# State-space block with a quantized feed-forward on one core: drives as float32 products with diagonals of B, and operands turned by transposing DMAs

## What is computed

```
# state-space part, per batch b, channel e (256), state n (16), time l (256)
xin = in_proj_w @ ctx.T ; u = silu(causal_conv4(xin) + conv_b)
dt_lo, B, C = x_proj_w @ u                       # 8, 16 and 16 rows
delta = softplus(dt_proj_w @ dt_lo + dt_proj_b)
state[e,n] = state[e,n] * exp(delta*A[e,n]) + (delta*u)[e] * B[n]   # over l
y[e] = sum_n state[e,n]*C[n] + D[e]*u[e]
x = x + tanh(g_xattn) * (y * silu(layernorm(x)))
# feed-forward part
t = layernorm(x); q = quantize per token (8 bits)
gate, up = q @ ternary(w_gate).T, q @ ternary(w_up).T
h = hadamard(silu(gate)*up)  (1024 wide);  q2 = quantize per token
x = x + tanh(g_ffn) * (q2 @ ternary(w_down).T)
```

## Time and profile before

| what | us |
|---|---|
| median of 3 runs (lowest, highest) | 222.16 (221.88, 225.17) |
| the profiled execution, its own time | 223.4 |
| its span, from first to last instruction | 221.6 |
| busy PE / PEld | 167.9 / 136.7 |
| busy DVE | 188.3 |
| busy ACT | 172.8 |
| busy POOL | 148.5 |

### The profile page before, as it was taken

One profiled execution on the slowest core, in us unless ns is written; L12 is line 12 of the kernel. 1 busy time (PEld: TensorE's weight loads), 2 busy tenths in 40 slices (PEclk: granted clock), 3 DMA queues, 4 the chain that ended last, 5 costly groups with the idle time before them and its releaser, 6 DMA issues.

```text
span 221.6 us, 3745 instructions
## 1 busy us (share of the span) xinstructions
PE 167.9 (76%) x1216; PEld 136.7 (62%) x1216; DVE 188.3 (85%) x292; ACT 172.8 (78%) x302; POOL 148.5 (67%) x247
## 2 busy tenths in 40 slices
PE   2757475997897994979867968988587598677873
PEld 1535354796695984748757864877484487544751
DVE  3462889597999999999999899999979996889983
ACT  0699997799899989799879895999497630985373
POOL 1103039969787989999999999999995299510000
PEclk9965587579999999999999999999999999999999
DMA  4994000000000000000000000000000000000001
GB/s 77 315 355 165 1 0 1 0 4 0 0 3 0 0 3 0 0 4 0 1 0 4 0 0 27 0 3 23 0 1 4 24 0 27 0 0 0 24 27 47
DMA packets 8148, 6.33 MB, mean 29 GB/s; under 512 B 2202, under 2 KB 7874, under 8 KB 8130
## 3 DMA queue, kind: packets, MB, share of 16 engines
q1 hardware_dynamic: 7154, 6.02, 8.6%
q10 hardware_dynamic: 976, 0.09, 0.3%
HBM read 5.05 MB, written 1.05 MB: 28 GB/s over the span
## 4 chain that ended last, share of the span: by engine, by line
POOL 25%; DVE 11%; PE 11%; ACT 8%; issue 4%; POOLq 0%; DVEq 0%; ACTq 0%
POOL driveT L1413 7%; POOL wnat L1479 7%; POOL wnat L1478 7%; PE GP L601 2%; DVE wnat L1789 2%; ACT L1242 2%; PE PY L483 2%; PE BC L422 1%; DVE wnat L1792 1%; DVE wnat L1730 1%; DVE prod L1686 1%; DVE state L1609 1%; PE UP L422 1%; ACT xn L1163 1%; DVE wnat L1778 1%
## 5 line engine op out<-in xcount | busy, mean ns | idle before, releaser
L1413 POOL TENSOR_SCALAR driveT<-duT,BT 128x256 f32<-128x256 f32 x120 | 58.4, 506 | 14.6 <-ACT duT L1071 11.9
L1054 ACT ACTIVATE decay<-delta,zero_c,aneg 128x255 f32<-128x255 f32 x128 | 65.0, 588 | 0.1
L1686 DVE TENSOR_TENSOR prod<-state,BC 128x1024 f32<-128x1024 f32 x32 | 38.5, 1202 | 3.2 <-PE BC L467 2.7
L1609 DVE TENSOR_TENSOR_SCAN state<-decay,BC 128x512 f32<-128x512 f32 x30 | 36.4, 1212 | 2.0 <-ACT decay L1054 1.2
L1609 DVE TENSOR_TENSOR_SCAN state<-decay,UP 128x512 f32<-128x512 f32 x30 | 35.9, 1198 | 0.0
L483 PE MATMUL PY<-id,prod 128*128 128x128 f32 x256 | 33.0, 273 | 0.8 <-DVE prod L1686 0.5
L483 PEld LDWEIGHTS PY<-id,prod 128*128 128x128 f32 x256 | 28.7, 140 | 1.8 <-issue 0.8
L1478 POOL TENSOR_TENSOR wnat<-wnat 128x512 f32<-128x512 f32 x18 | 22.9, 1271 | 8.0 <-DVE wnat L1730 7.2
L422 PE MATMUL BC<-id,driveT 128*128 128x128 f32 x120 | 19.4, 286 | 8.2 <-POOL driveT L1413 4.4
L1479 POOL TENSOR_TENSOR wnat<-wnat 128x512 f32<-128x512 f32 x18 | 22.9, 1272 | 0.0
L422 PEld LDWEIGHTS BC<-id,driveT 128*128 128x128 f32 x120 | 14.4, 148 | 11.9 <-issue 5.5
(11 more groups left out here) (254 smaller groups left out, 392.0 us busy)
## 6 DMA issues: line engine op xcount, KB each, us to landing
wnat<-in_L_ffn_w_gate_dram SPq DMA_DIRECT2D x1, 1024.0 KB, 6.4
xs<-in_x_dram SPq DMA_DIRECT2D x1, 1024.0 KB, 8.8
wnat<-in_L_ffn_w_up_dram SPq DMA_DIRECT2D x1, 1024.0 KB, 11.2
wnat<-in_L_ffn_w_down_dram SPq DMA_DIRECT2D x1, 1024.0 KB, 11.2
out_dram<-ot SPq DMA_DIRECT2D x8, 128.0 KB, 1.7
ctxs<-in_ctx_dram SPq DMA_DIRECT2D x1, 384.0 KB, 3.8
ctxs<-in_ctx_dram SPq DMA_DIRECT2D x1, 128.0 KB, 2.8
inw<-n_L_xattn_in_proj_w_dram SPq DMA_DIRECT2D x1, 128.0 KB, 2.6
```

The lines of the kernel that those rows point to most:

```text
L1054: last = nc.scalar.activation(decay[:, m % RING, h, n, 1:L], delta[:, b % 2, h, 1:L], ACT.Exp, bias=zero_c[:], scale=aneg[:, h, NB * j + n ...
L1413: last = nc.gpsimd.tensor_scalar(driveT[:, m % RING, c, n], duT[:, b % 2, c], BT[:, b % 2, c, NB * j + n:NB * j + n + 1], 1.0, ALU.mult, A ...
L1609: nc.vector.tensor_tensor_scan(state[:, g % STATES, h].rearrange("p n l -> p (n l)"), decay[:, g % RING, h].rearrange("p n l -> p (n l)"), ...
L1686: nc.vector.tensor_tensor(prod[:, g % RING].rearrange("p h n l -> p h (n l)"), state[:, g % STATES].rearrange("p h n l -> p h (n l)"), PC. ...
```

## The change

1. *Drives.* For every quarter of a batch (four states) POOL builds with one `affine_select` diagonal matrices of B: 128 x 1024 floats, 16 such instructions in all (`diagonals`). `drive_rows` is now a float32 product of `duT` (stationary) with two diagonals at a time (moving, 256 columns), two such products per half and step. The 120 POOL multiplications and the 240 transposes go, and so does the separate way of steps 0 and 1 (`B_rows`, `copy_B`, `first_drive`).
2. *Turning.* The weights are clipped from below in SBUF (`weight_floor`, DVE, 128 x 2048 16-bit) and turned by SP's transposing DMAs from SBUF to SBUF (`turn_weights`), 512 KB each. The tokens (`turn_tokens`, 128 KB) and the rounded operand of the down product (`turn_down`, 256 KB) of batches 0, 1, 2 (down: 0, 1) go the same way. `weight_T`, `weight_out`, `tokens_T`, `tokens_out_early` and four of six `q2_T` with their copies go. Batch 3's tokens and the down operands of batches 2 and 3 are still turned by PE.
3. *Front.* Small loads move from SP to ACT's queue; x is loaded ahead of the gate weight; a table load moves under the first loads; the first tap is a Copy without the bias, which goes into the Silu; two Relu move to DVE; the sum of the weights' absolute values comes after softplus(0).
4. *Order.* `decays` counts per half, and the lists of all engines are new.

The core of the diff (setups, semaphore names and most of the new lists left out):

```diff
@@ SP
+            def turn_weights(m):
+                sp.wait_ge(dve_wq, m + 1)
+                sp.dma_start(wT[:, m].rearrange("p (k c) -> p k c", c=P), wq[:, m], transpose=True).then_inc(turned_w, 16)
+            def turn_tokens(f):
+                sp.wait_ge(dve_q, f + 1)
+                if f >= 1:
+                    sp.wait_ge(pe_up, LC * f)
+                sp.dma_start(qT[:].rearrange("p t h c -> p (t h) c"), q[:].rearrange("p t e -> p (t e)"), transpose=True
+                             ).then_inc(turned_q, 16)
+            def turn_down(f, t):
+                sp.wait_ge(dve_q2, LC * f + t + 1)
...
+                sp.dma_start(q2T[:, t], q2[:, t], transpose=True).then_inc(turned_d[t], 16)
+            turn_tokens(0)
+            turn_weights(0)
+            turn_weights(1)
+            turn_weights(2)
+            turn_down(0, 0)
+            turn_tokens(1)
+            store(0, 0)
+            turn_down(0, 1)
+            turn_down(1, 0)
+            store(0, 1)
+            turn_tokens(2)
+            turn_down(1, 1)
...
@@ PE
+            def drive_rows(m, h):
...
+                pe.wait_ge(act_duT, b + 1)
+                pe.wait_ge(pool_diagB, m * NB // PER + 1)
...
+                for c in range(LC):
+                    last = nc.tensor.matmul(drive_bank(h).rearrange("p (n c l) -> p n c l", n=NB, c=LC)[:, :, c, :],
+                                            duT[:, b % 2, c, P * h:P * (h + 1)], diagB[:, q, c, at:at + NB, :],
                                             start=True, stop=True)
...
             def gate(f, t):
-                pe.wait_ge(act_qT, f + 1)
+                pe.wait_ge(turned_q, 16 * (f + 1))
                 if f == 0 and t == 0:
-                    pe.wait_ge(dve_wT, 6)
+                    pe.wait_ge(turned_w, 16 * 3)
+                    pe.wait_ge(act_spread, 2)
                     pe.wait_ge(act_duT, 2)
...
+            drive_rows(12, 0)
+            drive_rows(12, 1)
+            accumulate(10)
+            gate(0, 0)
             C_rows(11)
             drive_rows(13, 0)
...
@@ POOL
+            def diagonals(n, i):
+                pool.wait_ge(act_BT, n + 1)
+                if n >= 1:
+                    pool.wait_ge(pe_drive, HALF * (STEPS * (n - 1) + (i + 1) * PER // NB))
+                nc.gpsimd.affine_select(diagB[:, i].rearrange("p c n l -> p (c n) l"),
+                                        BT[:, n % 2, i].rearrange("p c n -> p (c n)").unsqueeze(2).to_broadcast([P, LC * PER, P]),
+                                        [[0, LC * PER], [1, P]], ALU.is_equal, no_part, base=0,
+                                        channel_multiplier=-1).then_inc(pool_diagB, 1)
@@ DVE
+            def weight_floor(m):
+                dve.wait_ge(dve_wr, m + 1)
+                nc.vector.tensor_scalar(wq[:, m], wq[:, m], -1.0, None, ALU.max).then_inc(dve_wq, 1)
...
             times_C(10)
-            token_scale(0, dve_ln_link)
-            weight_out(4)
-            weight_out(5)
+            weight_floor(2)
             round_tokens(0)
             scan(12, 0)
             scan(12, 1)
             times_C(11)
```

More of the change, by code:

```diff
@@ L764, in _ @@
             in_proj(1, 1)
+            drive_rows(0, 0)
+            drive_rows(0, 1)
+            x_dbl(1)
+            drive_rows(1, 0)
+            drive_rows(1, 1)
+            dt_proj(1)
             drive_rows(2, 0)
             drive_rows(2, 1)
-            x_dbl(1)
             drive_rows(3, 0)
@@ L770, in _ @@
             drive_rows(3, 1)
-            dt_proj(1)
+            gate_T(0)
+            in_proj(2, 0)
             C_rows(2)
@@ L830, in _ @@
             du_T(2)
-            C_rows(12)
-            gate(0, 1)
-            x_dbl(3)
-            drive_rows(14, 0)
             drive_rows(14, 1)
+            up(0, 1)
             C_rows(13)
-            up(0, 0)
+            accumulate(11)
             drive_rows(15, 0)
-            up(0, 1)
             drive_rows(15, 1)
             C_rows(14)
-            accumulate(10)
+            accumulate(12)
             drive_rows(16, 0)
+            accumulate(13)
+            x_dbl(3)
             drive_rows(16, 1)
-            accumulate(11)
+            accumulate(14)
@@ L846, in _ @@
             C_rows(15)
-            accumulate(12)
             drive_rows(17, 0)
-            accumulate(13)
             drive_rows(17, 1)
-            accumulate(14)
-            dt_proj(3)
+            inter_T(0, 0)
             C_rows(16)
-            accumulate(15)
-            C_rows(17)
             drive_rows(18, 0)
             drive_rows(18, 1)
+            accumulate(15)
+            dt_proj(3)
+            C_rows(17)
+            hadamard_mm(0, 0)
             drive_rows(19, 0)
-            inter_T(0, 0)
+            accumulate(16)
@@ L860, in _ @@
+            C_rows(18)
             drive_rows(19, 1)
-            C_rows(18)
-            hadamard_mm(0, 0)
+            inter_T(0, 1)
+            gate_T(2)
             drive_rows(20, 0)
-            accumulate(16)
-            gate_T(2)
+            C_rows(19)
             drive_rows(20, 1)
-            C_rows(19)
+            down(0, 0)
+            drive_rows(21, 0)
             accumulate(17)
-            accumulate(18)
-            inter_T(0, 1)
-            drive_rows(21, 0)
-            C_rows(20)
@@ L889, in _ @@
             drive_rows(24, 0)
+            C_rows(22)
             accumulate(20)
             drive_rows(24, 1)
+            down(0, 1)
             accumulate(21)
-            q2_T(0, 1)
             C_rows(23)
+            drive_rows(25, 0)
+            up(1, 1)
             accumulate(22)
-            up(1, 1)
-            drive_rows(25, 0)
             drive_rows(25, 1)
-            down(0, 1)
             accumulate(23)
@@ L1083, in silu_u @@
                     act.wait_ge(dve_conv, 2 * (DC - 1))
-                    nc.scalar.activation(u[:, 0], conv[:], ACT.Silu, bias=zero_c[:]).then_inc(act_u, 1)
+                    act.wait_ge(ld_cb, 16)
+                    for h in range(HALF):
+                        last = nc.scalar.activation(u[:, 0, h], conv[:, h], ACT.Silu, bias=cb[:, h:h + 1])
+                    last.then_inc(act_u, 1)
                 elif n == 1:
@@ new lines, in _ @@
+            inter_out(0, 0)
+            decays(21, 1)
+            spread(3)
+            decays(22, 0)
+            softplus(3)
+            quant_down(0, 0)
+            rstd2(1)
+            decays(22, 1)
+            inter_out(0, 1)
+            decays(23, 0)
+            second_norm(1)
+            scale_tokens(1)
+            decays(23, 1)
+            gate_out(2)
+            decays(24, 0)
+            quant_down(0, 1)
+            for_silu()
+            silu_gate(1, 0)
+            silu_z(3)
@@ L1364, in _ @@
+            decays(30, 0)
+            scale_tokens(2)
+            decays(30, 1)
+            quant_down(1, 1)
+            for_silu()
             silu_gate(2, 0)
@@ L1906, in _ @@
             weight_round(0)
-            weight_round(1)
-            weight_out(0)
             scan(7, 1)
             times_C(6)
-            weight_out(1)
+            weight_floor(0)
+            weight_round(1)
             scan(8, 0)
@@ L1915, in _ @@
             scan(9, 0)
-            weight_round(2)
             scan(9, 1)
-            weight_out(2)
+            weight_floor(1)
+            residual(0)
             times_C(8)
-            residual(0)
-            weight_out(3)
             scan(10, 0)
```

640 lines of the change are left out of this document (280 added, 360 removed).

## The result

| kernel | median us (lowest, highest) | ratio, 95% interval | profiled span |
|---|---|---|---|
| before, beside the changed one | 223.66 (221.88, 225.86) | | 221.6 |
| changed | 241.25 (241.15, 242.23) | 1.0808 [1.075, 1.0866] | 239.5 |

The change makes the kernel 8% slower, where the forecast had 4%. Between the profiles lie 17.9 us. The profiles of the eighth and the ninth experiment were taken in executions over 1.5% above the fastest of their kernel, so their later milestones aren't set beside others.

A forecast was written before the change was run, and what follows sets the result against it. DVE was taken as the bound, with PE 94% full after the change. Terms -6.8 + 2.5 + 8.5 + 1.5 + 1.7 + 3 - 1 = +9.4 us gave 231.5 us against 222.16; range 219 to 245.

The forecast's parts named there:

- the tail: End of the kernel: the same but for the order of a few PE calls, 0 us (-1 to +1).
- the gap: Sign: a DVE gap of 5 us or more ahead of times_C(11), at step 12.
- the dip of the clock: After PE's idle time at gate(0, 0): lower granted clock makes two steps' drives twice as long, +1.5 us (0 to 4).
- the pace of the drives: Sign: drives show as 8 PE instructions a step, 0.215 us apart.
- Part 1: Drives: PE pays 1.73 us a step against 0.88, 94% full from gate(0, 0) on; +3 us (0 to 6) there.
- My upper end: Four turns ahead of gate(0, 0), in 256-byte rows: 6656 packets at 43 ns, 19.4 us with the landing.
- -6.8 up to the rounding of the tokens: Start to round_tokens(0), ending at 80.2 instead of 87.0 us; front gain of 4.2 us at times_C(2) included.
- the other turns and the crowding: After the stall: single turns +1.7 us (0 to 5); PE's fuller list +3 us (0 to 6).
- A: Rival: four turns cheap at 6.4 us, single turns inside their slack, time stays at 225 or 223 us; chance 0.20.
- C: Rival: turns slow, 19.4 us for the four, SP's queue feeding many small pieces, 245 us; chance 0.15.
- D: Rival: PE is the bound, drives at 0.27 instead of 0.215, +4, 236 us; chance 0.52 together with the forecast.
- B: Rival: faster, 217 us, four turns landing within about 5 us and PE's lists fitting without a gap; chance 0.13.

The follow-up runs named there:

- eighth: experiment 2's kernel with duT and the diagonals in bfloat16 instead of float32; four executions of 228.87, 232.98, 236.39 and 236.7 us.
- ninth experiment: Changed kernel with the edits of experiment 2, experiment 3, the ten useless transposes and POOL's wait for du together; 228.23 us, ratio 1.0191.
- experiment 5: Kernel before, with each of its 240 drive transposes made twice, to load PE alone; 228.5 us, ratio 1.0243.
- Experiment 10: experiment 2's kernel with gate(0,0), down(0,0) and gate(2,0) moved later in PE's list, behind calls the scans need; 225.71 us, ratio 1.0112.
- experiment 2: Changed kernel with SP turning the weights ahead of batch 0's tokens, and the third weight rounded and clipped earlier on DVE; 231.17 us, ratio 1.0361.
- Experiment 12: Changed kernel with one line more: SP waits for the gates' and A_log's small loads before starting the large loads; 237.93 us, ratio 1.0639.
- experiments 4: Changed kernel with POOL building the diagonals by a product of the identity with B instead of affine_select; 245.96 us, ratio 1.0995.
- experiment 7: Changed kernel with tanh_gates behind silu_u(0), ten useless transposes ahead of du_T(0), and POOL's first diagonals waiting for du; 239.45 us, ratio 1.0715.
- 6: Changed kernel with tanh_gates behind silu_u(0) and ten useless PE transposes ahead of du_T(0); 240.24 us, ratio 1.0745.
- experiments 1: Changed kernel with SP turning the three weights ahead of the tokens of batch 0; 236.55 us, ratio 1.059.
- experiment 3: Changed kernel with tanh_gates moved behind silu_u(0) in ACT's list; 240.92 us, ratio 1.0787.
- Experiment 11: Edits of the ninth experiment and Experiment 10 together, with SP holding the large loads until A_log has landed; 220.42 us, ratio 0.9877.

## Why the prediction was right and wrong

The time, 241.25 us, lies above the forecast's own range (226.6 to 238). By the profile the change cost 8.5 us more than the 9.4 foreseen: 5.2 up to the rounding, 1.0 in the stall with its clock, 0.9 in the loop behind it, 1.5 in the tail. Of the signs that were named, the gap, PE's wait for a DMA, the dip of the clock and the pace of the drives came. The first scan (31.8 for 26 to 28) and the end of `times_C(2)` (46.1 for 43) didn't.

*Right: what bounds.* POOL's 25% of the chain was misleading. POOL lost 40 us of work (I had about 28, with diagonals at 2 us; they took 1.18, near the lower bound), and no time came of it. One reading there was wrong, without effect on the sum: 64 us against 58 is busier than before, not "no busier".

*Right: the drives.* A half's four instructions start 0.215 apart, 0.86 in all, as foreseen. Part 1 said PE would be nearly full and cost a few us, not be the bound. Experiments 5 and 10 give 2.4 and 2.05 us behind `times_C(11)`, where I took 3 less 1. Ahead of it I took 2.5; experiment 5 had 3.6 for the same load on the old lists.

*Right: the place and the cause of the stall; slightly small: the price.* I had 9.5 us from rounding to `gate(0, 0)`; it was 10.7. That it came so near is partly luck: 9.5 was picked between 6.4 and 19.4, and no row gave it. My upper end had the number of pieces right: SP's queue took 11,008 packets more, though 1,088 of small loads had moved to ACT's queue, so 12,096 for 3.01 MB turned (2944 KB), 249 bytes each. It had the price of one wrong. The share of both queues together rose from 8.9% of 221.6 to 15.3% of 239.5 us of 16 engines, 271 us of engine time, some 22 ns a packet and not 43. With 22 the 6656 packets are 9.2 us, and with a landing of 1.7 they are 10.9. SP's issue time is no sure second cause: for one 512 KB turn by itself (experiment 2) it took 1.6 to 1.9 us, and only in a row 2.0 to 2.6, with the DMA engines full. No run separates the issue from the engines. (The Trainium skill, "Advanced Engine Details and Errata", section "X-Bar Transpose (TRN2)", has turns as fast as ordinary DMAs, by which it would have been 6.4; the trace doesn't agree, with at most 211 GB/s against the loads' 355.) With the clock (`gate(0, 0)` and `C_rows(11)` took 2.4 us for 1.25, the first drives behind them 1.45 for 1.03) 8.5 + 1.5 = 10.0 became 11.0.

*Wrong: the front, the step "-6.8 up to the rounding of the tokens".* Within it the sentence that failed is "The first tap loses the table load of 1.28 us ahead of it, so `u` comes at about 11.9". I costed the moved small loads at nothing and gave no reason. But they now started at the same time as 1 MB loads and took 3 to 7 us longer to land, and ACT was held in issuing them. `u` ended at 15.4. Experiment 12 shows this step at 3.7 to 3.9 us. With the loads in the right order `u` ends at 12.0, and the end of `times_C(2)` is 42.38, against my 41.8: of the 4.3 us missed up to there 3.7 are the loads.

*Wrong, same sum: what a POOL instruction does to DVE's.* I priced the diagonals by POOL's time only. In the front they cost DVE 2.2 us (experiments 4 and 7); and `weight_floor(2)`, whose two sisters took 0.69 and 0.67 as I had it, took 2.47 beside two diagonals, 1.8 more, so that the saving of 1.6 us there vanished. That second one wasn't tested by itself, it is read from the trace; in experiment 2 that call moved away and took 0.69, but the rounding behind it then took 1.03 instead of 0.41, beside the same diagonals. The three slow instructions cost 1.6 us at the first scan (experiment 7 against 6). Experiment 12, which has them too, is late by only 1.0 us at the first scan (28.04 for 27.0) and by 0.6 at `times_C(2)`, so something else there must have come out better than I had it. From there to the rounding the forecast had -0.1 and the profiles show +0.7. With 1.8 for the floor the crowding of PE there must have cost some 1 us less than my 2.5, which no run singles out.

*Roughly right: the other turns and the crowding*, 4.6 for 3.7. Experiment 2 has 5.0 there. Experiment 10 takes 2.9 of them away (waits for turns, for which I took 1.7) and leaves 2.05 (the crowding, for which I took 2).

*Wrong by 1.5: the tail.* On the chain of the changed kernel in order of time (start us, us, what):

```profile
210.32 3.37 PE BC L636 x16
```

These 16 instructions take 3.36 to 3.60 us in the changed kernel and in experiments 1 and 12, where the tail is 39.2 to 39.5, and 2.05 us in the kernel before and in all other experiments, where it is 37.8 to 37.9. The granted clock is 0.66 from 211.5 to 215.5 us in the changed kernel and stays at 1.00 around the same products in experiment 3. So 1.3 of the 1.5 us are PE at the lower level, for which the forecast had nothing in the tail. What brings it in three kernels and not in the others wasn't tried: the wait of PE ahead of these products is 1.10 us in both.

*The rivals.* A (cheap turns) and C (slow ones) fell with 10.7 us against 6.4 and 19.4; the time is near C's 245, but not by C's mechanism. D fell: the pace of the drives is 0.215 (its +4 us didn't follow from 96 us against 94 either, that makes 2). B, faster, with 217 us, needed turns under 5 us and didn't come. Experiment 11 comes nearest, with 220.42, by another door: single turns were as slow as ever, but the scans no longer waited for them.

## What to carry to other kernels

In this kernel a DMA transpose was cheap only where its source was ready early and nothing urgent stood behind its consumer in an ordered list: put each turn in its queue when its own source is ready, and the product that needs it behind the work that doesn't. Let the small loads that the first instructions need land before the megabytes start: here that one wait was worth 3.3 us. When work moves to an engine whose instructions hold up those of the critical one, as POOL's did DVE's here, price that too, and not only their own time.

## What the runs showed of the hardware that was not expected

- *Small loads beside large ones.* 16 KB took 2.7 us to land when issued ahead of the 1 MB loads, 9.5 beside them, 3.4 to 3.6 when these were held back; loads of 1 KB 8.4 to 9.6 against 3.1 to 3.5. Issuing one took ACT 1.6 us instead of 0.5.
- *Issue time of a turning DMA.* 1.2 us of SP's queue for 128 KB, 1.6 to 1.9 for 512 KB by itself and 2.0 to 2.6 in a row; landing 2.4 and 3.0 us for 128 and 256 KB, 4.2 for 512 KB by itself and 4.7 in a row.
- *Less work on PE, lower clock.* With 16-bit drives PE was 22 us less busy, and the mean granted clock was 0.910 in the fastest execution and 0.89 to 0.90 in the others, where experiment 2 has 0.94 to 0.97.
- *The pace of `in_proj(1, 1)`*, 1.88 or 3.3 to 3.6 us after the same idle time of PE, with or without an edit ahead of it. In experiment 3 the granted clock's record stands at full beside 3.60 us, and also beside the 3.74 us of `in_proj(1, 0)`, where the changed kernel has the same 3.74 us with a record of 0.50. So the record can miss the lower level, and the duration tells. What sets the pace stays open.
